# Another merged order of two lanes' steps in a two-layer perceiver kernel

## The reference

```python
x = x + _L0_xattn_ref(_layernorm(x), ctx_1024, ...)   # one head, softmax over 257 keys
x = x + _L0_attn_ref(_layernorm(x), ...)              # 16 heads of 16, causal over 32 tokens
x = x + _L0_ffn_ref(_layernorm(x), ...)               # quantised, 1024 inner, silu(gate) * up
x = x + _L1_xattn_ref(ctx_1024, _layernorm(x), ...)   # 16 heads of 16, over the 257 keys
x = x + _L1_attn_ref(_layernorm(x), ...)              # 16 heads of 64, over 32 tokens
x = x + _L1_ffn_ref(_layernorm(x), ...)               # 8 experts, 2 chosen for a token, and a shared one
```

## Time and profile before

| | |
|---|---|
| median of three runs | 2981.65 us |
| profiled execution, its own time | 2995.97 us |
| its span, first to last instruction | 2993.7 us |
| mean granted clock of TensorE | 0.942 |
| busy: TensorE, VectorE, ScalarE, GpSimd | 80%, 61%, 40%, 16% |
| first half, 31 slots | 104.82 to 1737.10 us, from `hq_ps` to `hq_ps` |

### The profile page before, as it was taken

One profiled execution on the slowest core, in us unless ns is written; L12 is line 12 of the kernel. 1 busy time (PEld: TensorE's weight loads), 2 busy tenths in 40 slices (PEclk: granted clock), 3 DMA queues, 4 the chain that ended last, 5 costly groups with the idle time before them and its releaser, 6 DMA issues.

```text
span 2993.7 us, 94094 instructions
## 1 busy us (share of the span) xinstructions
PE 2390.6 (80%) x35446; PEld 1819.3 (61%) x35479; DVE 1816.4 (61%) x4744; ACT 1208.3 (40%) x3016; POOL 493.8 (16%) x614
## 2 busy tenths in 40 slices
PE   2788888888888888888888867888888888758882
PEld 2565666666566666666666656666666666646661
DVE  4566666666666666666666664566555555545555
ACT  1445555555555555455554551222222222212220
POOL 2111111111111111111111111111111111112220
PEclk9899999999999999999999988999999999979996
DMA  5011111111111111111111122000000000112225
GB/s 195 28 42 56 42 56 34 49 49 42 56 42 56 34 50 49 42 56 42 56 33 42 57 93 87 14 16 14 14 16 16 16 16 16 66 50 67 67 67 193
DMA packets 86060, 152.29 MB, mean 51 GB/s; under 512 B 11224, under 2 KB 39904, under 8 KB 84576
## 3 DMA queue, kind: packets, MB, share of 16 engines
q1 hardware_dynamic: 73136, 117.81, 12.5%
q0 software_dynamic: 6528, 17.87, 1.6%
q10 hardware_dynamic: 6192, 13.38, 1.2%
HBM read 120.40 MB, written 28.62 MB: 50 GB/s over the span
## 4 chain that ended last, share of the span: by engine, by line
issue 50%; PE 24%; DVE 9%; POOL 7%; ACT 4%; DMA 3%; DVEq 2%; SPq 0%; POOLq 0%; ACTq 0%
PE ps L385 16%; POOL mem L469 3%; PE ps L1193 2%; PE ps L1508 2%; POOL x L1065 2%; POOL rstd L1059 1%; PE ps L1145 1%; DVEq L1486 1%; DVE mem L1377 1%; DVE mem L1556 1%; DMA y_tok<-mem 1%; DVE mem L1351 1%; DVE mem L1407 1%; DVE mem L1408 1%; DVE mem L1411 1%
## 5 line engine op out<-in xcount | busy, mean ns | idle before, releaser
L791 ACT ACTIVATE mem<-ps 128x512 f32<-128x512 f32 (+6 forms) x800 | 436.6, 559 | 543.5 <-PE ps L385 260.7
L385 PE MATMUL ps<-mem 128*128 128x256 f16 (+1 forms) x4224 | 557.4, 290 | 119.0 <-DVE mem L1377 79.6
L385 PEld LDWEIGHTS ps<-mem 128*128 128x128 f16 x4224 | 422.3, 103 | 221.8 <-DVE mem L1377 83.1
L385 PE MATMUL ps<-xt,mem 128*128 128x128 f16 x4608 | 281.4, 220 | 29.0 <-DVE xt L1332 29.0
L385 PEld LDWEIGHTS ps<-xt,mem 128*128 128x128 f16 x4608 | 262.3, 98 | 42.4 <-DVE xt L1332 38.9
L841 ACT ACTIVATE mem<-ps,neg_max 128x257 f32<-128x257 f32 x512 | 237.4, 476 | 71.4 <-DVE neg_max L1028 71.4
L1059 POOL TENSOR_TENSOR rstd<-var_eps,neg_half 128x1 f32<-128x1 f32 x128 | 70.1, 548 | 1002.4 <-DVE var_eps L895 1002.4
L469 POOL TENSOR_TENSOR mem<-mem 128x514 f16<-128x514 f32 x136 | 160.7, 1184 | 368.3 <-ACT mem L464 368.3
L1028 DVE TENSOR_REDUCE neg_max<-ps 128x2 f32<-128x514 f32 x256 | 173.5, 688 | 58.4 <-PE ps L686 54.5
L1508 PE MATMUL ps<-mem 128*128 x576 | 156.5, 395 | 35.2 <-ACT mem L1534 34.7
L699 PE MATMUL ps<-cst,mem 128*128 128x128 f32 x1024 | 159.4, 284 | 12.5 <-ACT mem L841 12.5
(11 more groups left out here) (252 smaller groups left out, 4252.1 us busy)
## 6 DMA issues: line engine op xcount, KB each, us to landing
mem<-in_ctx_t SPq DMA_DIRECT2D x136, 257.0 KB, 2.7
mem<-in_ctx_n SPq DMA_DIRECT2D x136, 256.0 KB, 3.3
mem<-x_sorted SPq DMA_DIRECT2D x74, 128.5 KB, 2.1
mem<-y_pairs SPq DMA_DIRECT2D x32, 256.0 KB, 3.9
mem<-in_experts ACTq DMA_DIRECT2D x7, 768.0 KB, 8.7
x<-in_x_tok SPq DMA_DIRECT2D x34, 128.0 KB, 2.9
x_mid<-x SPq DMA_DIRECT2D x32, 128.0 KB, 1.7
x<-x_mid SPq DMA_DIRECT2D x32, 128.0 KB, 2.0
```

The lines of the kernel that those rows point to most:

```text
L385: last = pe.matmul(dst, a, b, start=i == 0 and j == 0, stop=i == n - 1 and j == 2)
L791: act.activation(dst, src, ACT.Copy).then_inc(*did(done))
```

## The change

Ten strings of letters are others: the lists of all five engines in the slots of the first half, those of TensorE, ScalarE and VectorE in the joining slot, and those of TensorE and VectorE in the slots of the second half. No instruction and no wait is added or taken away. The core of the diff:

```diff
 ORDER = {
     "first": dict(
-        tensor=("oooooyoyoyoyoooyooyoyoyooyoyyooyoooooyooyoooyoooooooooyoyyyoy"),
+        tensor=("oooooyoyooyyoooyooyoyoyoyoyyooyooyoyoyooooooooooyoyyoooyoyooo"),
...
-        gpsimd=("yyoooyooyyo"),
-        sync=("yyyyoyyoyyo"),
+        gpsimd=("yoyooyyoooy"),
+        sync=("yoyoyoyyyyy"),
     ),
...
     "second": dict(
-        tensor=("ooyyyoyoyyyyyoyoyo"),
+        tensor=("oyoyyyyoyoyyyoyyoo"),
...
-        vector=("yyyyooyoyoooooyyoooyooyooooyyoooyyooyoooooooo"),
+        vector=("yyyyoyoyoooyooyoyoooyooyoyoooooyoyooyoooooooo"),
```

More of the change, by code:

```diff
@@ L181 @@
     "first": dict(
-        tensor=("oooooyoyoyoyoooyooyoyoyooyoyyooyoooooyooyoooyoooooooooyoyyyoy"),
-        scalar=("oooyooyyoooyoyoooyoyoooyoooyyoooyoooyoyyooooooyyy"),
-        vector=("yoyyyyoooooyyooyyyoooooyoooooyoyyyyyoyooyyooyyoyyoyooyyoyyyyyyyyyyyyyoooyyyyyyyyyyo"),
-        gpsimd=("yyoooyooyyo"),
-        sync=("yyyyoyyoyyo"),
+        tensor=("oooooyoyooyyoooyooyoyoyoyoyyooyooyoyoyooooooooooyoyyoooyoyooo"),
+        scalar=("ooooyoyyoooyooyooyyoooyooyoooyyooyoyyoooooyooyyoo"),
+        vector=("yoyyyyooooooyyyoyyoooyoooooooyoyyyyyyooyyooyyoyyyooyyoyyyyyoyyyyyyyoyyyyyoooyyyyyyo"),
+        gpsimd=("yoyooyyoooy"),
+        sync=("yoyoyoyyyyy"),
     ),
     "between": dict(
-        tensor=("ooooooyoooooooyooyoyoyoyyooyoyooyooooooyoooooooooooo"),
-        scalar=("yoooyooyyooyoyooooooooooooooooyoyoooyoyoooyyyy"),
-        vector=("yyyoyyyooooooyoooooooyoooooyoyoyoyooyoyyoooyyyoyoooyoy"),
+        tensor=("oooooooyoyoooyooooyoyoyoyoyyooyooooooooooooooyoooooo"),
+        scalar=("yoooyooyyyooyoooooooooooooooooooyoooyoyooyyyyy"),
+        vector=("yyyyoyyyooooooyooooooooyooooyooyoyoooyooyyooyyyyyoooyo"),
         gpsimd=("yoooooo"),
```

## The result

The changed kernel takes **3110.24 us** (median of 4 runs, 3107.65 to 3112.51); the kernel before, measured beside it, takes 2984.11 (4 runs, 2981.3 to 2994.62). The ratio is 1.0406, with a 95% interval from 1.0384 to 1.0427. The forecast was 3070, with a range from 3005 to 3125.

The account below looks back on a forecast made before the run. The prediction took TensorE, busy 80% of the span, as the bound, with order changing only its idle time and clock. Terms 12 + 51 + 3 + 28 = +94 us gave 3075 from the median, written as 3070 us, range 3005 to 3125.

Parts of the forecast that it names:

- +12 us of idle time: First half: TensorE's changed waits add 0.4 us a slot over 31 slots, between -4 and +28 us.
- +51 of clock: First half: more half-clock stretches behind TensorE's idle places, 1.1 x 1.5 us x 31 slots, bounds 0 and +98.
- I take two slow stretches a slot: First half: two half-clock stretches a slot after the change, where there were 0.9.
- the forecast's upper bound: First half, clock: three slow stretches a slot, +98 us.
- the pair of 1.8: First half: TensorE's waits of 0.4 and 1.4 us ending before `pl_ps`, said to slow the clock in six of 31 slots.
- in series with the load that this chunk's end allows: Joining slot: ScalarE's split of weight chunk 3, about 2 us, moves behind the last `pt4_f`; +3 us, between 0 and +6.
- +0.9 us a slot, +28 us: Second half: `self5_y` inherits GpSimd's scatter wait through `xn5` between the two `o5_lo`; range +15 to +53 us.
- reach further down than up: Whole sum: the least trusted clock term's errors were said to lean downward, so 3075 was written as 3070 us.
- The clock falls no oftener: First-half rival: TensorE's split stalls cause no more slow clock than before; 3025 us, chance 0.2.
- Faster: Rival: the younger lane's chain reaches `xq` 2.1 us earlier, first half -1.3 us a slot; 2970 us, chance 0.06.
- The scatter lands earlier: Second-half rival: `xn5` holds nobody, so that half is unchanged; 3045 us, chance 0.08.
- Nothing: Whole-kernel rival: first-half gains pay for the second half, nothing measurable; 2982 us, chance 0.05.

Follow-up runs that it names:

- e7: The kernel before plus 16 unread 128x256 matmuls per first-half tile before the wait for `xn2`: 2950.94 us, ratio 0.9874.
- e8: The changed kernel plus unread matmuls before `xn2`, `p2_norm`, `sel` (12, 16, 12) and 30 behind `o5_ps` in the second half: 3135.12 us, ratio 1.0497.
- e9: The changed kernel plus unread matmuls before `xn2`, `p2_norm`, `sel` (12, 16, 12) and 16 of 128x512 before second-half `xn5`: 3045.3 us, ratio 1.0176.
- e5: The kernel before with only GpSimd's first-half list as in the changed kernel: 2964.83 us, ratio 0.9921.
- e2: The kernel before with only the joining slot's three lists taken from the change: 3005.22 us, ratio 1.0035.
- e4: The changed kernel with second-half `xn5` again behind both `o5_lo` and `xt_ps5` behind `self5_y`: 3083.75 us, ratio 1.0314.
- e10: The kernel before with GpSimd's changed first-half list, 10 unread 128x256 matmuls before `xn2` and 18 behind `o5_ps`: 2984.89 us, ratio 0.9974.
- e11: The kernel before with GpSimd's changed first-half list and 18 unread 128x256 matmuls behind `o5_ps`, none added in the first half: 2920.12 us, ratio 0.9767.
- e12: The kernel before with GpSimd's changed first-half list, 5 unread 128x512 matmuls before `xn2` and 9 behind `o5_ps`: 2899.22 us, ratio 0.9691.

## Why the prediction was right, and where it was off

**The first half: right, in both of its terms.** Forecast were +12 us of idle time and +51 of clock, 63 together; measured were 61.5. The filled kernels split that. Without slow clock the slots of before take 51.35 us (e7) and those of the change 51.80 to 51.85 (e8, e9): 0.45 to 0.5 us a slot, 14 to 15 us, against the "+0.4 us, 31 slots: +12 us". This is an upper bound, as e8 and e9 have 0.4 us a slot of waits for "issue". The clock takes 1.3 us a slot before and 2.8 after, a difference of 1.5 and thus at least 47 us, against +51.

The size of the clock term holds luck. "I take two slow stretches a slot" was met by 62 stretches in 31 slots, but time at half clock is 3.5 times that of before (321 and 92 us), which with stretches as long as those of before would have been about three a slot, the number behind the forecast's upper bound. And "each costs 1.5 us" holds for neither kind of slot: against 51.8, the two short stretches of a 53.7 us slot cost 1.9 together, the long and the short one of a 55.5 us slot 3.7. The long ones run on across the idle time before `self_y`; TensorE stands idle for 24 of the 164 us of the sixteen. The working of the forecast also has the pair of 1.8 slow the clock in six slots of before; it did so in four, and in the first two of the six one longer stretch lay behind `xn2` alone.

One reading failed in part: `xn` was to be always at 0.41 us in the first half, and its mean is 0.51 there (200 to 1700 us) in the changed kernel; in e5, where GpSimd's list alone is moved, it is 0.41.

**The joining slot: the mechanism was half right, and the term was mis-sized.** The text had the split of chunk 3 "in series with the load that this chunk's end allows", +3 us within 0 to +6. Measured were +12.75, or +11.1 in e2 alone. The split came 15.5 us later and not 2; the move itself gives about 4 of these, and the rest comes from TensorE's own lateness, 3 from its first wait and most of the others from the wait of 2.99 us for an earlier `lo_part` and the slow clock behind it. And the harm is not at the last chunk: VectorE's list holds two splits ahead of `sel`, so `y4_ps` waits 7.83 us instead of 1.58, while the wait for the last chunk, which was to grow, fell from 5.53 to 2.69. The step that failed is that ScalarE's move was priced on ScalarE's queue alone, without what stands behind the waiting instruction on VectorE, and that the new lists of TensorE and VectorE in this slot were priced at nothing.

**The second half: the mechanism was right, and the term was too small.** Forecast was +0.9 us a slot, +28 us; measured were 1.44, +43.2 in 30 intervals. The idle time was met: 4.36 us now, 2.52 + 0.93 before, so +0.9. The rest is the clock, which the forecast kept only for its upper end ("if the longer idle time slows more matmuls"): half-clock time rises from 116 to 205 us, and half of these 89 us, 1.5 a slot, is the most it can cost. In the slot shown the 24 matmuls take 4.78 us (4.21 before) and `xt_ps5` 0.69 (0.38). e4 gives `xn5` 1.03 us of the 1.44; the other 0.4 stays when `xn5` is put back, so it comes with other moves, which the forecast had priced at nothing.

**The sum.** Term by term in us, forecast and measured: first half +63 and +61.5, joining slot +3 and +12.75, second half +28 and +43.2, ends 0 and -1: 94 and 116.5. Of the 40 us by which 3070 was too low, 22.5 are these. 5 were taken off because the clock term's errors "reach further down than up", which they did not. The other 12 or so lie in the reference: the sum was made against a profiled execution 14 us above the median, while that of the changed kernel lies at its median.

**The rivals.** (1) *The clock falls no oftener*, 3025 us: refuted by 62 stretches in place of 25, and by e8 and e9, where work in the same idle times gives 2.8 us a slot back. The rule of the Trainium skill on which it leaned (TensorE: Matmul & The Clock Gate, "Why this matters for your kernels", no idle gaps above about 3 us) does not hold here: 2.38 us are followed by 0.50, and so are 1.77 by 0.56, while 1.87 in the same slot are followed by 1.00, and in the next slot the last two are the other way round. So in this kernel the length of a gap alone does not decide it. (2) *Faster*, to be decided by the 1.8 us before `y4_ps`: they are there, 1.77. One of its gains is real all the same, GpSimd's list gives 23 us by itself (e5); the rest of the change outweighs it. (3) *The scatter lands earlier*: no, GpSimd waits 2.09 us for it still. (4) *Nothing*: no.

## What to carry to other kernels

Where one engine runs a fixed list, price a reordering by the idle places it makes, one by one, and read from windows of several slots what the clock does behind each kind; here idle time and clock were some 14 and 47 us of the same edit. An idle time that cannot be removed can be filled with unread matmuls, which gave 37 and 46 us here in the two halves of the old kernel, but with few and wide ones: the same work in twice as many instructions lost nearly all of it again. And it has to be looked at afterwards where the clock falls then, as it can fall behind the next wait. And a step moved on one engine has to be followed to the engine whose list waits for it, and to what stands behind that wait.

## What was not expected of the hardware

- **Matmuls added to one loop can make another wait.** e10 differs from e11 by ten more matmuls a tile in the first loop alone, and in the second, which is the same, the instruction queue moved 99 packets instead of 1 (1900 to 2500 us) and TensorE waited 2.2 and 1.8 us for issue in every second slot. With half as many matmuls of twice the width (e12) there is no such wait, at 86 us less (2984.89 and 2899.22).
- **A slow clock moves on to the next wait.** With the wait for `xn2` cut from 2.3 to 1.5 us (e5), the stretches at half clock went from 25 to 35, 30 of them behind a pair of waits of 0.4 and 1.4 us that had brought 4 before. With the wait for `xn2` filled at its old length (e7), the same pair brought one.
- **Slow stretches merge.** A second wait of 0.5 us within a slow stretch came with one of 10.2 us, in 16 slots of 31, where nearly all had been 3.4 before.
